# Last pass of the token network: a step's first transposes and their copy, moved behind the first dense layer of the step's second half

## The reference

```python
for i in range(LAYERS):                       # 4 layers, 32 channels
    x1 = spectral_conv(h, w1, w2)             # 12 x 24 modes kept
    x2 = einsum('bchw,oc->bohw', h, conv_w[i]) + conv_b[i]
    h = layer_norm(x1 + x2, ln_g[i], ln_b[i]) # over the 32 channels
    if i < LAYERS - 1:
        h = gelu(h)
h = gelu(h @ fc1_w + fc1_b)                   # 32 -> 128
h = gelu(h @ fc2_w + fc2_b)                   # 128 -> 64
h = h @ fc3_w + fc3_b                         # 64 -> 1
```

## Time and profile before

| | us |
|---|---|
| median of 3 runs | 3734.32 |
| lowest, highest | 3724.97, 3740.9 |
| the profiled execution, its own time | 3736.74 |
| its span | 3734.8 |
| granted TensorE clock, mean of the span | 0.931 |
| busy in the span: PE, DVE, ACT, POOL | 3185.0, 2446.6, 2205.7, 2144.3 |

### The profile page before, as it was taken

One profiled execution on the slowest core, in us unless ns is written; L12 is line 12 of the kernel. 1 busy time (PEld: TensorE's weight loads), 2 busy tenths in 40 slices (PEclk: granted clock), 3 DMA queues, 4 the chain that ended last, 5 costly groups with the idle time before them and its releaser, 6 DMA issues. The chain is left out here.

```text
span 3734.8 us, 201691 instructions
## 1 busy us (share of the span) xinstructions
PE 3185.0 (85%) x86496; PEld 2194.0 (59%) x86496; DVE 2446.6 (66%) x3804; ACT 2205.7 (59%) x3597; POOL 2144.3 (57%) x1147
## 2 busy tenths in 40 slices
PE   7998598888679888768888858999999968888887
PEld 4776477777557777646777643434333326666665
DVE  7897468888368888547888724444444436677675
ACT  5776156666246666436666616777777744455454
POOL 2543368888268888447888714444444425555553
PEclk9999679999779999969999979999999988999898
DMA  3443345555335555335555431121212110000000
GB/s 103 143 138 127 100 136 163 163 163 161 102 117 165 163 163 163 118 102 161 163 163 162 133 104 52 54 59 50 59 53 59 56 36 9 11 11 11 11 11 9
DMA packets 220274, 366.77 MB, mean 98 GB/s; under 512 B 108723, under 2 KB 137971, under 8 KB 219843
## 3 DMA queue, kind: packets, MB, share of 16 engines
q1 hardware_dynamic: 216354, 360.29, 32.4%
q0 software_dynamic: 3744, 3.84, 0.7%
HBM read 206.31 MB, written 157.71 MB: 97 GB/s over the span
## 5 line engine op out<-in xcount | busy, mean ns | idle before, releaser
L1248 POOL TENSOR_TENSOR rstd<-var,mhalf 128x16 f32<-128x16 f32 x512 | 1542.4, 3030 | 947.6 <-DVE var L1026 947.6
L1040 DVE TENSOR_TENSOR zt<-ps,rstd 128x512 f32<-128x512 f32 x512 | 352.4, 688 | 383.6 <-POOL rstd L1248 377.7
L558 PE MATMUL ps<-d,hp 128*32 128x48 f32 x32768 | 478.4, 212 | 67.5 <-ACT asb L785 35.9
L558 PEld LDWEIGHTS ps<-d,hp 128*32 128x32 f32 x32768 | 405.3, 113 | 169.6 <-issue 69.9
L1026 DVE TENSOR_REDUCE var<-sq 128x16 f32<-128x528 f32 x384 | 404.1, 1053 | 42.1 <-ACT sq L745 42.1
L785 ACT COPY asb<-ps 128x384 f32<-128x384 f32 x512 | 253.5, 495 | 284.4 <-PE ps L558 284.2
L466 PE MATMUL ps<-zb,ex 48*128 48x512 f32 x1024 | 314.8, 685 | 105.2 <-DVE zb L1086 103.6
L533 PE MATMUL ps<-ident,hp 128*128 128x128 f32 x2048 | 377.9, 309 | 13.0 <-ACT ho L769 10.8
L483 PEld LDWEIGHTS ps<-cwl,hc 64*64 64x64 f32 x16384 | 280.8, 143 | 149.2 <-issue 139.3
L494 PEld LDWEIGHTS ps<-dyi,gt 64*48 64x48 f32 x16384 | 236.8, 126 | 218.2 <-issue 199.7
L494 PE MATMUL ps<-dyi,gt 64*48 64x32 f32 x16384 | 280.0, 213 | 97.3 <-ACT gt L809 58.4
(11 more groups left out here) (168 smaller groups left out, 4962.9 us busy)
## 6 DMA issues: line engine op xcount, KB each, us to landing
h_scratch<-ho SPq DMA_DIRECT2D x256, 512.0 KB
hc<-h_scratch SPq DMA_DIRECT2D x256, 512.0 KB, 4.4
wsb<-in_w SPq DMA_DIRECT2D x64, 288.0 KB, 4.0
g_scratch<-gs SPq DMA_DIRECT2D x192, 96.0 KB, 2.3
gin<-g_scratch SPq DMA_DIRECT2D x256, 72.0 KB
gin<-g_scratch SPq DMA_DIRECT2D x512, 36.0 KB
tokens<-wsb SPq DMA_DIRECT2D x256, 4.0 KB
xin<-in_x SPq DMA_DIRECT2D x64, 48.0 KB
```

The lines of the kernel that those rows point to most:

```text
L558: last = nc.tensor.matmul(a_ps[row:row + 32, 2 * TRIG * k:2 * TRIG * k + 2 * TRIG], hp[b][:, u, 8 * j + k].rearrange("p v r -> p (v r)"), ...
L1040: nc.vector.tensor_tensor(by_px(zt[h][:, u]), by_px(main_ps(s, h, u)), scale, ALU.mult).then_inc(norm_ready, 1)
L1248: nc.gpsimd.tensor_tensor(rstd[u][:], var[u][:], mhalf[:], ALU.pow).then_inc(rstd_ready, 1)
```

## The change

Within a step of the last pass, `turn_last(c, 0)` on PE and `affine(c, 0)` on ACT leave the end of the half with `k` = 0. They now stand in the half with `k` = 1: on PE between `fc1_rows(heads, 1)` and `widen`, on ACT between `gelu1(heads, 1)` and the squares. The second group, `turn_last(c, 1)` and `affine(c, 1)`, stays last in the step. No instruction is added or removed, the waits inside each helper are the same, and the lists of DVE, POOL and SP are untouched (line numbers behind L705 shift by 2, behind L895 by 4).

```diff
@@ PE, last_pass @@
                             fc1_rows(*heads, k)
                         if k == 0 and (d := where(i, p, h, 3)):
                             fc3_rows(*d)
+                        if k == 1 and c:
+                            turn_last(*c, 0)
                         if k == 1 and behind(i, p, h, 0, 2):
                             widen(s, p, g, h)
                             conv(s, p, g, h)
@@
                         if nxt:
                             i1_last(1 - p, *nxt, k)
-                        if c:
-                            turn_last(*c, k)
+                    if c:
+                        turn_last(*c, 1)
@@ ACT, last_pass @@
                     for k in range(2):
                         if heads:
                             gelu1(*heads, k)
+                        if k == 1 and c:
+                            affine(*c, 0)
                         if k == 1 and behind(i, p, h, 0, 2):
                             square(s, 2 * i + p, h, 0)
                             square(s, 2 * i + p, h, 1)
                         if heads:
                             gelu2(*heads, k)
-                        if c:
-                            affine(*c, k)
+                    if c:
+                        affine(*c, 1)
```

## The result

| | before | changed |
|---|---|---|
| median of 4 runs | 3737.61 us | 3778.18 us |
| lowest, highest | 3724.97, 3745.84 | 3772.23, 3785.24 |
| ratio, 95% interval | | 1.0103 (1.0076 to 1.0129) |
| profiled execution, its span | 3736.74, 3734.8 | 3772.23, 3770.4 |
| clock, mean of the span | 0.931 | 0.931 |

A forecast was written before the change was run, and what follows sets the result against it. PE was taken to bound the last pass at full clock. Per step 0.64 - 0.08 + 0.03 = 0.59, rounded down to 0.57, over 62 steps gave 35 us more: forecast 3770 us, range 3752 to 3785.

The forecast's parts named there:

- What bounds: In the last pass PE sets the pace at full clock, busy 756.06 of 840 us, so each PE gap counts.
- Term 1: Dense layer L662 with k = 1, freed from the transposes, starts 0.08 us a step sooner, bounds 0 and 0.14.
- Term 2: First transposes, moved between L662 and L466 where PE never idles, cost 0.64 us a step, ends 0.57 and 0.71.
- Term 3: ACT's copy, moved behind gelu1, delays the squares that follow conv: 0.03 us a step, out of 0 to 0.08.
- The sum: Last pass: 0.59 us a step, rounded down to 0.57; over 62 steps 35 us slower, bounds 27 and 49.
- (A): Room behind the dense layer is free, PE waiting for gelu1 before the second dense layer: 3729 us, chance 0.07.
- (B): Dense layer starts as soon as L494 ends, the wait for the normalisation vanishing whole: 3707 us, chance 0.03.
- (C): Dense layer inherits the wait for POOL through DVE's L1092, so Term 1 vanishes: 45 us, 3779 us, chance 0.10.
- (D): Clock falls in the pass; if every fourth step fell, 41 us on top of 35: 3810 us, chance 0.04.

## Why the prediction was right, point by point

**What bounds.** Right. PE's gaps decided. The sum was made of where an idle stretch opens and where one doesn't, and the trace shows these places.

**Term 1, the dense layer that moves forward.** The mis-sized term. I took 0.08 us a step, with ends of 0 and 0.14; it is 0.17. The step that failed is the choice of the distance behind `gelu2`: I took 0.25 us because of the register instructions ahead of the layer. Measured are 2515.97 - (2514.73 + 1.11) = 0.13 us, and in the other step 2502.94 - (2501.68 + 1.11) = 0.15. Behind DVE's copies it is as little as 2502.94 - (2502.41 + 0.48) = 0.05, not 0.15. The bound of 0.14 failed by that last distance. In the first of the two steps the working gives 2510.57 + 0.05 = 2510.62, which is 0.24 us sooner than 2510.86 and not 0.14, and in the second 0.14. The trace agrees: before, the first parts of four steps in turn are 5.88, 6.08, 5.96 and 6.09 us, and in the changed kernel they are 5.83 and 5.84 in turn, so the two steps that I had read gained 0.24 and 0.13, and the mean over all is 0.17. That the layer would inherit the wait for the normalisation through DVE's queue was right in kind (34 of its waits end there), but `gelu2` ends within 0.1 us of DVE's copies, and with the chain shortened, cut or bypassed in three different ways the step fell by 0.01 us.

**Term 2, the transposes that move back.** Right: 0.64 us, with no idle at the second dense layer. The second part of the step grew by exactly that, and it did so behind conv as well.

**Term 3, the copy on ACT.** I took 0.03 us out of 0 to 0.08; it is 0. In the changed kernel the squares start 2507.02 - (2505.71 + 1.16) = 0.15 us after conv's end, the same distance as before. The working added the durations of instructions that overlap.

**The sum.** 0.57 us a step against 0.47 measured; 35 us against 31 for the pass. The profiled execution came out at 3772 us as summed, but that is luck. Term 1, with the 0.03 us of Term 3, made the 59 regular steps 7 us too dear (59 x 0.57 = 34 against 27). The steps with the text's instructions and the first one came out 2 us dearer than in the sum, which had nothing of their own for them, and some 5 us of spread lie ahead of the pass. The median of 3778 us is a third number, and its interval of 28 to 48 us holds both 31 and 35.

**Rivals.** (A) PE has no idle at the second dense layer in the changed kernel. (B) the hole is 0.9 us, and taking the wait for the normalisation away gives 0.19 us a step, not 0.44. (C) in every second step the chain of roots does end last, but by no more than the 0.02 us between 5.84 and 5.82; in the others it has 0.19 us left. (D) the clock fell only at the pass's start and in the steps with the text's instructions, as before. I had read it once there, but in the kernel before two of those three steps had matmuls at the lower level (17.2 and 15.7 us against 14.2). In the changed kernel the dense layer waits 2.55 us in each of the three. Behind the first wait the clock stayed (a step of 14.55 us), behind the other two it fell (17.72 and 17.75), which is 3.2 us for a fall where I had 2.7. These are the first and the third:

```profile
2285.88 1.14 PE L662 MATMUL ps<-ho,fc 32*128 32x512 f32 x8 [2.55 <-DVE zb L1096]
...
2318.15 1.31 PE L662 MATMUL ps<-ho,fc 32*128 32x512 f32 x8 [2.55 <-DVE zb L1096]
2319.39 1.12 PE L543 MATMUL ps<-ident,zt 128*128 128x128 f32 x4
2320.44 2.08 PE L466 MATMUL ps<-zb,ex 48*128 48x512 f32 x4
```

Why the same wait is followed by a fall in some of these steps and not in others stays open. The regular steps with their hole of 0.9 us run at clock 1.00, as this window of the changed kernel shows:

```profile
2500.00:2700.00 200.00, 179.04 (x2756) 75.92 (x2752) 84.08 (x155) 137.54 (x154) 88.22 (x31) 1.00 0.18 52
```

The Trainium skill's remark that transposes count differently as PE activity ("TensorE: Matmul & The Clock Gate", Part 4) has no effect that this stretch could show.

## What to carry to other kernels

Before moving work out from behind a wait, ask what the work behind it waits for on its own account: here the dense layer was held by a gelu and a copy until 0.17 us before it had started anyway, so the transposes were filling a hole that stayed open. Moving filler from a hole to a stretch without idle costs its whole length, less the little that the hole closes. The gain to be had from such a wait can be measured by making the awaited chain shorter in the old order, before anything is moved.

## What the runs showed of the hardware that I had not expected

- ACT starts an instruction 0.11 us before the listed end of the one before: a copy of 0.78 us took a slot of 0.67 us, two gelus of 2.12 us a slot of 2.01 us.
- A group of two 128 x 128 float32 transposes takes 0.42 us of PE and a group of four 0.64 us, in the same place between the same neighbours. An estimate from these two sizes is 0.20 us for the group and 0.11 us for each.
- Between the end of its last releaser and the start of a matmul group lay 0.05 us (DVE's copies; 0.15 in rows 6) to 0.15 us (ACT's gelu) at the second dense-layer group of a step. At the step's start PE's idle was 0.27 us in every second step and 0.15 us in the others, in the same positions of the loop in every kernel. What makes that difference was not tested.
